# Cross stage of a decoder layer: keys folded in pairs for the top-32 search, score copies ahead of exponentials, a new order at the last tile

## The reference

```
scores = einsum('bthd,bghd->bhtg', Q, K) / sqrt(32)
topv, topi = top_k(scores, 32)                 # the 32 largest of 2048, per token and head
probs  = softmax(topv)
attn   = zeros_like(scores).at[.., topi].set(probs)
c_t    = attn.mean(heads) @ (x_vision @ Wv)
scale_in, shift_in   = split(c_t @ W_film_in + b_film_in)      # "film"
x = layernorm(x_text) * (1 + gate * scale_in) + gate * shift_in
y = s4d(x)            # a long convolution over each sequence, by FFT, plus a skip term
y = y * (1 + gate * scale_out) + gate * shift_out
```

## Time and profile before

| what | value |
|---|---|
| median of 3 runs | 4802.67 us (4802.39 to 4808.14) |
| the profiled execution, its time | 4804.69 us |
| the profiled execution, its span | 4802.7 us |
| VectorE busy | 3799.6 us (79% of the span) |
| TensorE busy | 4064.0 us (85%) |
| ScalarE busy | 2066.0 us (43%) |
| GpSimd busy | 2187.5 us (46%) |
| first MAX8 of the cross function's first job starts | 984.48 us |
| last MAX8 of job 127 ends | 3145.53 us |
| feed-forward's first transfer is issued | 3304.64 us |

### The profile page before, as it was taken

How to read it: one execution, slowest core, us unless ns; L and a number is a source line. 1 busy time by engine, 2 the same in 40 slices (tenths; PEclk the granted TensorE clock), 3 DMA queues, 4 the chain that set the end, 5 groups by cost and what they waited for, 6 DMA issues and landing times. The chain is left out here.

```text
span 4802.7 us, 70845 instructions
## 1 busy us (share of the span) xinstructions
PE 4064.0 (85%) x28066; PEld 2950.6 (61%) x28066; DVE 3799.6 (79%) x4097; ACT 2066.0 (43%) x3816; POOL 2187.5 (46%) x2260
## 2 busy tenths in 40 slices
PE   8999994669899888988898889874889898998984
PEld 6777771346666566666666666664666666666652
DVE  5666667689999999999999999954557676676767
ACT  3333431134555545554454445421345454454543
POOL 1111114625555378777877787730334233342320
PEclk9999997758889889999999999987999999999996
DMA  2111115230001101111111211034421111111101
GB/s 88 47 48 51 47 43 196 46 104 30 31 32 40 61 29 36 47 62 34 34 38 43 64 31 38 29 106 161 138 74 57 35 57 57 52 50 50 53 22 38
DMA packets 214589, 276.01 MB, mean 57 GB/s; under 512 B 96659, under 2 KB 144403, under 8 KB 210224
## 3 DMA queue, kind: packets, MB, share of 16 engines
q1 hardware_dynamic: 196850, 216.91, 14.9%
q0 software_dynamic: 17408, 54.56, 3.1%
HBM read 186.44 MB, written 84.98 MB: 57 GB/s over the span
## 5 line engine op out<-in xcount | busy, mean ns | idle before, releaser
L1592 POOL TENSOR_TENSOR c_s<-c_s,c_z 128x2048 f32<-128x2048 f32 x128 | 580.1, 4532 | 549.7 <-ACT c_z L1370 546.3
L1913 PE MATMUL f_p_g<-f_hT,f_w 128*128 128x128 f32 x4096 | 534.1, 294 | 66.7 <-ACT f_gT L2013 52.2
L1533 DVE MAX8 c_top<-c_z 128x8 f32<-128x2048 f32 x256 | 585.0, 2285 | 4.4
L1534 DVE MATCH_REPLACE8 c_z<-c_top,c_z 128x2048 f32<-128x2048 f32 x256 | 582.6, 2276 | 0.0
L1913 PEld LDWEIGHTS f_p_g<-f_hT,f_w 128*128 128x128 f32 x4096 | 522.7, 209 | 87.2 <-ACT f_gT L2013 55.1
L1251 PE MATMUL c_p_m<-c_wf,c_uT 128*128 128x512 f32 x768 | 415.0, 683 | 189.1 <-ACT c_yb L1424 165.5
L1180 PE MATMUL c_p_a<-c_diag,c_s 128*128 128x128 f32 x4096 | 491.8, 279 | 40.5 <-ACT c_diag L1384 40.5
L1180 PEld LDWEIGHTS c_p_a<-c_diag,c_s 128*128 128x128 f32 x4096 | 480.4, 195 | 62.0 <-ACT c_diag L1384 50.2
L1921 PE MATMUL f_p_o<-f_w,f_gT 128*128 128x512 f32 x1024 | 481.8, 592 | 0.0
L1378 ACT ACTIVATE c_s<-c_s,c_nb 128x2048 f32<-128x2048 f32 x128 | 256.4, 2003 | 448.4 <-POOL c_s L1592 448.3
L1251 PEld LDWEIGHTS c_p_m<-c_wf,c_uT 128*128 128x128 f32 x768 | 162.4, 220 | 411.5 <-issue 406.1
(11 more groups left out here) (362 smaller groups left out, 7655.0 us busy)
## 6 DMA issues: line engine op xcount, KB each, us to landing
mod_out<-c_fo POOLq DMA_DIRECT2D x32, 512.0 KB, 2.9
f_mr<-mod_out SPq DMA_DIRECT2D x32, 512.0 KB, 4.7
p_ct<-in_ctxT SPq DMA_DIRECT2D x16, 768.0 KB, 5.0
c_vals<-in_ctx SPq DMA_DIRECT2D x4, 3072.0 KB, 11.7
c_kb<-kspec SPq DMA_DIRECT2D x22, 512.0 KB, 3.3
a_xt<-in_xT SPq DMA_DIRECT2D x32, 256.0 KB, 3.1
a_xr<-in_x SPq DMA_DIRECT2D x32, 256.0 KB, 2.6
x<-a_out POOLq DMA_DIRECT2D x32, 256.0 KB, 2.5
```

The costliest lines, as they stand in the source:

```text
L1533: st.link(v.max(best[n], work))
L1534: st.link(v.match_replace(work, best[n], work, NEG))
L1592: pool.tensor_tensor(row, row, low, ALU.subtract).then_inc(cut_ready, 1)
L1913: last = mm(p_g[:, f % 8, :], w1[:, k, f * P:(f + 1) * P], hT[:, k * P:(k + 1) * P], start=(k == 0 and f % 4 == 0), stop=(k == KD - 1 and ...
```

## The change

VectorE folds the row first: upper is the larger and lower the smaller of key k and key k + 1024, both 1024 wide. It seeks the 32 largest of upper (four MAX8) and the 16 largest of lower (two MAX8), merges lower's 16 with places 17 to 32 of upper by an elementwise maximum against the reversed list, and takes the 32nd largest as the least of these and of place 16 (thr). The first eight instructions of a job use behind(), which waits not for the instruction just issued but for the one before it; the rest use link(). ScalarE's tb is made from thr.

ScalarE copies scores ahead of the exponentials in two places of a tile, and copies the slot ahead of weigh(j+2). GpSimd's store_mod comes before cut(j), finished moves from the end of its tile to between the first cuts of the next one, transform and convolved move one cut later, and copy_f waits for the end of convolved (halved) in place of finished. The last slot moves behind film(TILES-1, 1), with its copy and its store; the last film and ScalarE's copies for it move ahead of the last attention products, and on GpSimd the last cut moves behind modulate(TILES-2) and store_mod(TILES-2).

```diff
+    def behind(self, ins):
+        self.mark(ins)
+        at_least(self.eng, self.sem, self.base + self.n - 1)
...
-        work, low = z[:, 0, :], z[:, 1, :]
+        upper, lower, low = z[:, 0, 0:N2 // 2], z[:, 0, N2 // 2:], z[:, 1, :]
+        other = [second[:, 8 * n:8 * n + 8] for n in range(2)]
...
@@ vector @@
-                st.link(v.max(best[0], row))
-                st.link(v.match_replace(work, best[0], row, NEG))
-                for n in range(1, 4):
-                    if n == 2 and j:
-                        invert(j - 1)
-                    if n < 3:
-                        st.link(v.max(best[n], work))
-                        st.link(v.match_replace(work, best[n], work, NEG))
-                v.max(best[3], work).then_inc(z_done, 1)
+                st.mark(v.tensor_tensor(upper, row[:, 0:N2 // 2], row[:, N2 // 2:], ALU.max))
+                st.behind(v.tensor_tensor(lower, row[:, 0:N2 // 2], row[:, N2 // 2:], ALU.min))
+                st.behind(v.max(best[0], upper))
+                st.behind(v.max(other[0], lower))
+                st.behind(v.match_replace(upper, best[0], upper, NEG))
+                st.behind(v.match_replace(lower, other[0], lower, NEG))
+                st.behind(v.max(best[1], upper))
+                st.behind(v.max(other[1], lower))
+                if j:
+                    invert(j - 1)
+                for n in range(1, 3):
+                    st.link(v.match_replace(upper, best[n], upper, NEG))
+                    st.link(v.max(best[n + 1], upper))
+                late = top[:, par, 16:32]
+                st.link(v.tensor_tensor(late, late, second[:, ::-1], ALU.max))
+                v.tensor_reduce(thr[:, par:par + 1], top[:, par, 15:32], AX.X, ALU.min).then_inc(z_done, 1)
@@ scalar @@
-                a(tb[:, par:par + 1], top[:, par, 31:32], ACT.Copy, scale=STEEP).then_inc(tb_ready, 1)
+                a(tb[:, par:par + 1], thr[:, par:par + 1], ACT.Copy, scale=STEEP).then_inc(tb_ready, 1)
...
-                    at_least(act, v_ready, g - NCB)
+                    at_least(act, halved, g - NCB)
...
                 if t + 1 < TILES:
                     copy_s(t + 1, 0, 0)
+                if t + 1 < TILES:
+                    copy_s(t + 1, 0, 1)
                 weigh(j + 1)
                 diagonal(j + 1)
-                if t + 1 < TILES:
-                    copy_s(t + 1, 0, 1)
...
-                weigh(j + 2)
                 if slot_job(t) is not None:
                     copy_slot(t)
-                diagonal(j + 2)
                 if t + 1 < TILES:
                     copy_s(t + 1, 0, 3)
+                else:
+                    copy_fi(TILES - 2)
+                weigh(j + 2)
+                diagonal(j + 2)
+            copy_fo(TILES - 2)
             below(LAST)
-            copy_fi(TILES - 2)
             weigh(LAST)
             diagonal(LAST)
-            copy_fo(TILES - 2)
-            copy_slot(TILES)
...
             copy_fo(TILES - 1)
+            copy_slot(TILES)
@@ tensor @@
-                    at_least(pe, slot_copied, slots(t + 1))
+                    at_least(pe, slot_copied, slots(min(t + 1, TILES - 1)))
...
+            film(TILES - 2, 1)
             attn(LAST - 1)
-            film(TILES - 2, 1)
             attn(LAST)
-            slot(TILES)
...
             film(TILES - 1, 1)
+            slot(TILES)
@@ gpsimd @@
                 else:
                     pool.wait_ge(k_out, 16 * NCB)
+                    at_least(pool, v_ready, g - NCB)
...
                 if t > 1:
                     modulate(t - 2)
+                    store_mod(t - 2)
                 cut(j)
-                if t > 1:
-                    store_mod(t - 2)
+                if ready and not of_kernel(ready):
+                    finished(t - 1)
+                cut(j + 1)
                 if job is not None:
                     transform(t)
-                cut(j + 1)
+                cut(j + 2)
                 if job is not None and not of_kernel(job):
                     convolved(t)
-                cut(j + 2)
-                if job is not None and not of_kernel(job):
-                    finished(t)
                 if t < NCB:
                     skip(t)
-            cut(LAST)
             modulate(TILES - 2)
             store_mod(TILES - 2)
+            cut(LAST)
+            finished(TILES - 1)
             modulate(TILES - 1)
@@ sync @@
-            store_y(slot_job(TILES), TILES)
...
             load_rest(2)
+            store_y(slot_job(TILES), TILES)
```

More of the change, by code:

```diff
@@ L918, in cross @@
         tb = m.sb("tb", [P, 2])
+        thr = m.sb("thr", [P, 2])
+        second = m.sb("second", [P, 16])
         den = m.sb("den", [P, 2])
@@ L968, in cross @@
          dve_step, dft_in, fb_in, kd_in, kb_in, skipped, f_done, f_copied, slot_done, slot_copied, f_step, spec_ready,
-         prod_ready, v_ready, fb_ready, g_in, ig_in, rf_done, rf_copied, r_step, rk_read, rv_ready, ri_done,
+         prod_ready, halved, v_ready, fb_ready, g_in, ig_in, rf_done, rf_copied, r_step, rk_read, rv_ready, ri_done,
          ri_copied) = [
@@ L975, in cross @@
                 "dve_step dft_in fb_in kd_in kb_in skipped f_done f_copied slot_done slot_copied f_step spec_ready "
-                "prod_ready v_ready fb_ready g_in ig_in rf_done rf_copied r_step rk_read rv_ready ri_done "
+                "prod_ready halved v_ready fb_ready g_in ig_in rf_done rf_copied r_step rk_read rv_ready ri_done "
                 "ri_copied").split()]
@@ L1207, in slot @@
                 if t == TILES:
-                    pe.wait_ge(fo_copied, TILES - 1)
+                    pe.wait_ge(fo_copied, TILES)
                 else:
@@ L1646, in convolved @@
                 idft8_head(pool, fs, fw[:], fz[:], ft[:])
+                pool.sem_inc(halved, 1)
             def finished(t):
@@ L1650, in finished @@
                 at_least(pool, slot_done, NCB + i)
-                tmp = fz[:, 0, 0:4].rearrange("p (i r) c -> p i r c", r=2)
+                tmp = fw[:, 0, 0:4].rearrange("p (i r) c -> p i r c", r=2)
                 idft8_tail(pool, fs, ft[:], fv[:], tmp).then_inc(v_ready, 1)
@@ L1655, in _ @@
                 job = forward_job(t)
+                ready = t and forward_job(t - 1)
                 masked_identity(t)
```

## The result

The changed kernel takes 4734.8 us (median of 4 runs, 4710.1 to 4738.7) against 4805.4 us (4 runs). The ratio is 0.984, with an interval of 0.981 to 0.988: 1.6% faster. The forecast was 4591 us with a range of 4555 to 4675; the sign held, and a gain of 71 us came where 212 were forecast. The profiled execution took 4733.5 us for a span of 4731.5.

The account below looks back on a forecast made before the run. The prediction took VectorE's searches to set the pace, with late score copies adding 43 us. Gains of 195 us from the search, 16 from waits and 1 from moved work sum to 212, giving 4591 us, range 4555 to 4675.

Parts of the forecast that it names:

- The search's price: VectorE's search: 15.02 us a job in place of 16.55, a gain of 195 us over 128 jobs.
- its two bounds: Search time: 15.02 us if the first eight instructions' ends are hidden, 15.84 if none is.
- rival 2: Data tiles: GpSimd, slowed by VectorE's two-input fold, becomes the bound; 4664 us, half of it 4627; chance 0.20.
- whether the cut's duration varies: Sign for GpSimd slowed by the fold: the cut's duration of 4.53 us and whether it varies.
- data tiles over 64 us: Sign that the prediction is wrong: data tiles over 64 us, or a job over 15.9.
- The chain of the second pair: Data tiles, GpSimd, ScalarE and TensorE up to the fourth score copy: 58.3 us for four jobs, which have 60.1.
- the price of the lower clock: TensorE's 32 products before attn(j-1): 3.3 us more, chain 61.6; VectorE waits 1.5 us a tile, half taken, 17 us.
- The wait at turn: TensorE stands at turn(t+1) for about 3.4 us while copy_fo waits for weigh(j-1).
- The reading of the kernel before: Searches of the kernel before: VectorE sets the pace, late score copies add 43 us, TensorE and GpSimd have time to spare.
- the wait for the slot copy: TensorE before its film products: the wait of 7.8 us a tile for the slot copy is gone.
- The tail behind the last search: End of the kernel, moved work: a gain of 1 us, bounded by a gain of 4 and a loss of 5.
- The forecast's own band: Whole kernel: 4562 to 4625 us for searches of 15.0 to 15.3 us and waits of 0 to 50; chance 0.60.

Follow-up runs that it names:

- linked run: Changed kernel with 14 zero-adding products ahead of turn(t+1), and link() in place of behind() in the search's first eight instructions: 4734.6 us, against 4628.5 with behind().
- contention taken away: Changed kernel with the fold replaced by one-input copies of the row's two halves by MATCH_REPLACE8 (output not the reference's): 4599.4 us, ratio 0.956.
- copy_fo first: Changed kernel with ScalarE's copy_fo, copy_s(t,1,1) and copy_x ahead of weigh(j-1) and diagonal(j-1): three runs 4758 to 4766 us, one 4667.
- one-input fold in the old order: One-input copies in place of the fold (output not the reference's), in the order of the kernel before: 4750.1 us, ratio 0.989.
- The new search in the old order: Kernel before with only the new search and thr, none of the new order: 4834.1 us, ratio 1.0055.
- two reordered kernels: Changed kernel with copy_fo, copy_s(t,1,1), copy_x ahead of weigh(j-1): 4758 to 4766, once 4667 us; same with copy_u behind below(j+2): 4662 to 4668, once 4767.
- filled kernel: Changed kernel with 14 matrix products of a zero tile ahead of turn(t+1) in tiles 9 and up: 4628.5 us, ratio 0.964.

## Why the prediction was off

**The search's price** was right and a little high: 15.02 forecast, 14.80 measured. That the first eight hide their ends is worth 106 us, as the linked run shows, and the forecast took the right one of its two bounds.

**The step that failed** is rival 2, as the prediction put it: the two-input fold was allowed to slow GpSimd alone, at a chance of 0.20, and the sum took nothing for it. The runs show that it slows both, each by about 1 us where they meet. On VectorE that is 4.3 us in each data tile, and 94 us over all searches: 2088.8 us, less 128 x 14.80 = 1894.4, less 101 of waits. No term stood for this. The rival's own price, 4664 us at full size, would have been short too. And the sign named for it, whether the cut's duration varies, could not tell it: the cut went from 4.53 to 4.56 us, since most cuts start as a fold has ended, while L1662 nearly doubled. The sign that spoke was the other one, data tiles over 64 us. The Trainium skill's "GPSIMD Engine Reference", section "Key points", which the prediction cited beside the rival, names this very case; the trace agrees, at 1.23 us growing to 2.05 to 2.29 on VectorE, and 0.32 to 0.46 growing to 1.30 to 1.44 on GpSimd.

**The chain of the second pair** was the right one to watch, and its cover of 1.8 us as thin as said, but its sum took low(j+1) as made 2.24 us after z_done(j+1), had no term for low(j+2), and took the price of the lower clock as 3.3 us on one group of products. All three are off. low(j+1) is ready 6.7 us after z_done(j+1) (2080.8 to 2087.5), because copy_s(t,1,3) stands ahead of it in ScalarE's queue, and low(j+2) 6.5 us after z_done(j+2), because of copy_s(t+1,0,1) and copy_u. From the attention products to the end of the fourth copy, 13.15 in the sum, it takes 17.7 (2067.66 to 2085.39). The stretched instructions lengthen the chain on GpSimd by 1.9 us in transform and 1.8 in convolved. The wait at turn was forecast rightly, 3.4 against 3.35; the fall of the clock behind it was taken as half likely and comes in each tile, twice. So the loop closes on itself at 68.27. Waits came to 101 us, of which 4.74 in each of 20 data tiles; the forecast had 27. Together: 94 + 74 of waits, less 28 for the cheaper search, are the 139 us that the 2088.8 lie above the forecast's searches of 1949.6, up to rounding. The 3 us left to the profiled execution are the tail (2.5) and small differences elsewhere.

**The reading of the kernel before** had VectorE setting the pace in all tiles, with copies that come 43 us too late in all. That holds for the kernel tiles. In the data tiles the old order takes 68.2 us even with a search of 14.9 and no contention, so what set their length was already a loop that the search is not in, and the waits were the little by which it exceeded the search.

**Right by its own steps:** the wait for the slot copy is gone. VectorE's waits moved to the second pair. The kernel tiles wait 0.2 to 1.6 us in four of eight (1.2 in each of the eight forecast). With contention taken away, the forecast of 4591 is 8 us from what was measured, 4599; what was missing is mainly the contention and what follows from it. That the two are so close is partly luck: that run's searches have two value loads more each, and its data tiles still wait.

**Small ones that were off.** The tail behind the last search takes 160.6 us where it took 159.1 (a gain of 1 forecast). The forecast's own band of 4562 to 4625 doesn't follow from its conditions: 15.3 us a search and 50 us of waits give 4650. The measured time lies above either.

**What stays open.** Before, after, and two more kernels (copy_fo first, and the one-input fold in the old order) have data tiles of 68.27 us although their work differs by several us. The new search in the old order has another fixed value, 71.7. In all five the clock falls in each data tile, once in the three with the old order and twice in the two others, at the same place each time; where it falls in some tiles only, tiles of 60.4 and 62.3 appear. That the fall itself holds the length at one value was not tested. Nor is it known why executions of the two reordered kernels split into 4662 to 4668 and 4758 to 4767 us, or why one of the changed kernel took 4710.

## What to carry to other kernels

Before a VectorE instruction with one input is replaced by one with two, look at what GpSimd does at that moment: a fold in the middle of its transforms cost both engines up to a microsecond an instruction, while in the two tiles without a transform it cost nothing, since the cuts began as the fold had ended, and in the kernel tiles 0.3 to 0.4 us a tile. When VectorE's work is cut so that its pace comes within two microseconds of the next loop, walk that loop with every in-order queue in it, also for instructions that are late only because another one ahead of them is. And if TensorE stands in each round and the clock falls behind it, as after 3.35 us here, try a few products that add zero, no more than fit the wait: 14 gave back 106 us, 30 gave back 48.

## What was not expected of the hardware

The 128 x 16 instruction, 0.17 us alone, took 1.21 us beside a GpSimd instruction of 128 x 1024 and ended with it: the hold-up lasts as long as what the other engine is doing, not in proportion to one's own size. And TensorE at 97% busy in the filled kernel finished the same work in 106 us less than at 94%.
